# Sandwich of attention and channel mixing on one core: the gate read out of PSUM one slot sooner, ahead of the low plane of probabilities, its statistics and power one slot sooner too

## The reference

```
def ln(x): return (x - mean(x)) / sqrt(var(x) + 1e-5)

# attention, full 2048 x 2048 scores per batch
n = ln(x)
qkv = n @ weight_qkv         # bands 0:64 and 192:256 of the 256 in float16, 64:192 in float32
q, k, v = split(qkv); q = q / 16
y = softmax(q @ k.T) @ v
x = x + ln(y @ out_w.T + out_b)

# channel mixing
n = ln(x); prev = n shifted down by one row, zeros in the first
r = sigmoid((mu_r * n + (1 - mu_r) * prev) @ W_r.T)
k = square(relu((mu_k * n + (1 - mu_k) * prev) @ W_k.T))
x = x + ln(r * (k @ W_v.T))
```

## Time and profile before

| | |
|---|---|
| median of 3 runs | 855.45 us (854.24 to 855.83) |
| the profiled execution, its own time | 853.94 us |
| its span in the trace | 851.8 us |
| TensorE busy | 794.6 us, 93% |
| VectorE busy | 712.5 us, 84% |
| GpSimd busy | 550.8 us, 65% |
| ScalarE busy | 508.5 us, 60% |

### The profile page before, as it was taken

How to read it: one execution, slowest core, us unless ns; L and a number is a source line. 1 busy time by engine, 2 the same in 40 slices (tenths; PEclk the granted TensorE clock), 3 DMA queues, 4 the chain that set the end, 5 groups by cost and what they waited for, 6 DMA issues and landing times.

```text
span 851.8 us, 16118 instructions
## 1 busy us (share of the span) xinstructions
PE 794.6 (93%) x5749; PEld 572.5 (67%) x5749; DVE 712.5 (84%) x1805; ACT 508.5 (60%) x639; POOL 550.8 (65%) x717
## 2 busy tenths in 40 slices
PE   4879999999999999999999999999999999998664
PEld 3536767677776777677776776777777777777542
DVE  5698989988899998988889998988888888874553
ACT  3475556566566557766656557666666656655341
POOL 2110245677668777777768767777777777788761
PEclk9999999999999999999999999999999999999865
DMA  7565777477756864686648756775456646585100
GB/s 179 112 148 107 161 174 147 101 145 150 150 88 166 172 143 110 134 155 147 133 93 169 166 137 130 137 155 131 106 111 136 119 109 108 137 157 139 41 25 26
DMA packets 369312, 109.72 MB, mean 129 GB/s; under 512 B 342992, under 2 KB 368976, under 8 KB 369232
## 3 DMA queue, kind: packets, MB, share of 16 engines
q1 hardware_dynamic: 369232, 108.69, 61.0%
HBM read 18.75 MB, written 8.39 MB: 32 GB/s over the span
## 4 chain that ended last, share of the span: by engine, by line
PE 52%; DVE 30%; issue 8%; POOL 5%; ACT 2%; DMA 1%; SPq 1%; DVEq 0%; POOLq 0%; ACTq 0%
DVE probs L849 7%; PE M L1058 4%; PE M L1060 4%; PE M L1059 4%; PE S L1090 4%; PE S L1091 4%; PE S L1092 4%; PE S L1093 4%; PE S L1094 4%; PE Y L1111 4%; PE Y L1112 4%; PE Y L1113 4%; PE Y L1114 4%; PE Y L1115 4%; DVE p_lo L865 3%
## 5 line engine op out<-in xcount | busy, mean ns | idle before, releaser
L849 DVE TENSOR_SCALAR_CACHE_REDUCE probs<-S 128x512 f32<-128x512 f32 x256 | 173.2, 677 | 29.7 <-PE S L1094 29.5
L647 ACT ACTIVATE probs<-probs,exp_bias,kappa 128x2048 f32<-128x2048 f32 x64 | 133.6, 2088 | 51.3 <-DVE exp_bias L860 50.8
L865 DVE TENSOR_TENSOR p_lo<-probs,p_hi 128x2048 f16<-128x2048 f32 x64 | 151.5, 2367 | 3.1 <-ACT p_hi L597 3.1
L1112 PE MATMUL Y<-pt_lo,planes 128*128 128x256 f16 x512 | 140.2, 274 | 0.0
L1111 PE MATMUL Y<-pt_hi,planes 128*128 128x256 f16 x512 | 140.2, 274 | 0.0
L1113 PE MATMUL Y<-pt_hi,planes 128*128 128x256 f16 x512 | 140.2, 274 | 0.0
L1114 PE MATMUL Y<-pt_lo,planes 128*128 128x256 f16 x512 | 140.1, 274 | 0.0
L1115 PE MATMUL Y<-pt_hi,planes 128*128 128x256 f16 x512 | 140.0, 273 | 0.0
L597 ACT ACTIVATE p_hi<-probs 128x2048 f16<-128x2048 f32 x64 | 121.5, 1899 | 21.8 <-DMA pt_lo<-p_lo 21.8
L1090 PE MATMUL S<-turned,q_hi 128*128 128x512 f16 x256 | 97.9, 382 | 8.2 <-DVE q_lo L840 5.1
L541 POOL TENSOR_TENSOR xm_lo<-mixed,xm_hi 128x512 f16<-128x512 f32 x62 | 99.9, 1611 | 4.2 <-ACT xm_hi L597 4.1
(11 more groups left out here) (184 smaller groups left out, 2005.9 us busy)
## 6 DMA issues: line engine op xcount, KB each, us to landing
x_res<-in_L_attn_x SPq DMA_DIRECT2D x32, 256.0 KB, 3.0
out_x<-gate SPq DMA_DIRECT2D x32, 256.0 KB, 2.3
xs<-in_L_attn_x SPq DMA_DIRECT2D x28, 128.0 KB, 2.9
xs<-in_L_attn_x SPq DMA_DIRECT2D x14, 256.0 KB, 3.3
pt_hi<-p_hi SPq DMA_TRANSPOSE x64, 4.0
pt_lo<-p_lo SPq DMA_TRANSPOSE x64, 4.0
mxt<-mx SPq DMA_TRANSPOSE x31, 3.3
pt_hi<-in_L_attn_weight_qkv SPq DMA_DIRECT2D x3, 128.0 KB, 2.6
```

What stands on the lines that cost most here:

```text
L647: act.activation(probs[:, h % 2, t, :], probs[:, h % 2, t, :], ACT.Exp, bias=exp_bias[:, t:t + 1], scale=kappa[:, 0:1], accum_out=row_sum[ ...
L849: dve.tensor_scalar(probs[:, h % 2, t, c * BLK:(c + 1) * BLK], S[k % RING][:, :], 1.0, None, ALU.mult, ALU.max, accum_out=chunk_max[:, t, ...
L865: dve.tensor_tensor(p_lo[:, t, :], probs[:, h % 2, t, :], p_hi[:, t, :], ALU.subtract).then_inc(p_lo_made, 1)
L1112: pe.matmul(to[:, 0, :], low, p_l, start=False, stop=final, skip_group_check=True)
```

## The change

The constants of three stages become smaller by one, and the call of `gated` moves up in VectorE's list from behind the low squares to a place ahead of `probs_low`. `gate_norm`, `finish` and the store stay where they were.

```diff
     FEED = 58
-    GATE = 60
-    GATE_STATS = 61
-    GATE_RSQRT = 62
+    GATE = 59
+    GATE_STATS = 60
+    GATE_RSQRT = 61
     GATE_NORM = 62
...
                 if (h := at(k, Y_LOW)) is not None:
                     attended_low(h)
+                if (h := at(k, GATE)) is not None:
+                    gated(h)
                 if (ht := exp_at(k, FIRST_LOWER, LOWER)) is not None:
                     probs_low(*ht)
...
                 if (h := at(k, SQUARE_LOW)) is not None and h >= DRAIN:
                     squares_low(h)
-                if (h := at(k, GATE)) is not None:
-                    gated(h)
                 if (h := at(k, GATE_STATS)) is not None:
                     gated_stats(h)
```

## The result

The changed kernel takes 858.04 us (median of 20 executions, 854.17 to 859.38), the kernel before 853.62 us (20 executions on the same chip, 851.21 to 855.83). The ratio is 1.0052, 95% interval 1.0041 to 1.0063: 4.4 us slower, where I had forecast 13.3 us faster. The time lies outside my range, on the side that I gave 5 in 100. All medians of this document are over fast executions; one of the six executions of the kernel "old order in the drain" took 4688 us and is not among them.

The account below looks back on a forecast made before the run. Bound: PE, losing 9.1 us in the 17 half-units with preparation, mainly to gate waits, plus long drain waits. 8.5 us there and 4.8 in the drain gave 13.3, so 855.45 to 842.2 us; stated range 839.0 to 850.5 (0.83).

Parts of the forecast that it names:

- What bounds the kernel: 17 half-units with preparation take 412.00 us where 402.9 would do: 9.1 us lost, mainly PE waiting for the gate.
- Part one: Gate ahead of tile 0's p_lo on VectorE: ends 3.0 us sooner, gap to the receptance 3.5 us instead of 0.5.
- Part two: Statistics and power sooner: gshift ahead of tile 1's p_lo, 3.6 us sooner; VectorE's 1.58 us wait before y_lo goes.
- What it costs: Power ahead of L520 and differences on GpSimd: 0.75 us VectorE cost per half-unit against 0.7 room; gain taken as 8.5.
- the third rival: L520 and L526 both ahead of tile 1's p_lo, 2.2 us per half-unit: 10.7 us slower, 866; chance 0.05.
- The drain: From slot 256 on, shorter PE waits and a faster clock: 4.8 us gain, bounds 2.7 and 8.5.
- The two waits that I had counted on: Project waits at slots 265 and 281: first to gain 2.3 us; second, together with slot 285's gate wait, 2.3.
- term (d): Drain receptance waiting 1.17 us for xm_lo: either gains 1.2 us or loses 0.6, taken as 0.
- Term (e): Drain: with shorter pauses fewer PE matmuls run at the slow clock, gain taken as 0.2 us.
- the drain gives nothing: Drain waits for the gate may turn into waits for xm_lo or rrstd: 847.0 us; chance 0.13.
- signs for "right": No gate waits before slot 256, half-units at 23.70 us, gshift 0.2 to 0.3, no y_hi wait, shorter drain project waits.
- signs for "wrong": Tile 1's p_lo over 3.2 us, PE waits at scores or project, half-units over 24, or rrstd waits over 1 us.

Follow-up runs that it names:

- old order in the drain: Changed kernel with GATE_RSQRT back at 62, and gate and statistics at their old place from half-unit 24 on: 847.0 us, ratio 0.9921 to the kernel before.
- the version with the power kept: Changed kernel with only GATE_RSQRT back at 62, so gate and statistics move but the power does not: 846.35 us, ratio 0.9918 to the kernel before.
- The two kernels above that keep this order and leave work out: Changed kernel with 2 of 256 columns of GpSimd's differences made: 845.1 us; changed kernel with 1408 of 2048 columns of tile 0's p_lo made: 847.1 us.
- power alone: Kernel before with only GATE_RSQRT at 61, the power ahead of mix_in_sum on GpSimd: 869.3 us, ratio 1.0188.

## Why the prediction was wrong, step by step

**What bounds the kernel: right.** 17 half-units, 9.1 us lost, and 402.9 us as the least: the version with the power kept has exactly that.

**Part one: right.** The receptance's matmul started at 622.96 in the steady half-unit, the gate was done at 619.47, 3.5 us ahead as forecast.

**Part two: the chain right.** gshift started 5.7 us behind the gate, where I had 6.0, took 0.20 us, and ScalarE did not wait for it there any more; p_lo of tile 1 started 7.4 us behind the gate, where I had 7.5. What I didn't say is what GpSimd does until its moments come: nothing, for 4.32 us.

**What it costs: this step failed**, in two terms. I had written 0.9 us of loss at tile 1 less 0.16 us won at tile 0, 0.75 against 0.7 us of room, and taken nearly the full gain. The loss at tile 1 came out smaller, 2.86 - 2.29 = 0.57 us. The gain at tile 0 was a loss of 3.11 - 2.47 = 0.64 us. Of this p_lo I had said in part one that it is 0.68 us later and that its readers are far off; I had not asked what GpSimd would start in those 0.68 us. I had read it in a half-unit without preparation, where xt is the neighbour, and carried it over to the 17 in which xm_lo is. Then the operations that GpSimd does later: L908 (21.0 - 15.8) / 17 = 0.30 us, L916 0.12. Together 1.63 us. The busy time of the stretch shows a little less: 400.4 - 378.2 = 22.2 us, and one p_lo more, of 2.7 us, starts 0.15 us behind its end: 1.31 to 1.46 us per half-unit. With that my own sum comes near: 22.2 to 24.9 us of cost less 12.8 us of room is 9.4 to 12.1 us of lag on 402.9, 412.3 to 415.0; measured 413.0. The 12.8 us, though, are 17 times 0.75, the figure of the cost; the room that I had worked out was 1.45 - 0.76 = 0.69 us, 11.8 us in the 17, and with it the sum gives 413.3 to 416.0.

It is the third rival, the port that takes more than the gate gave, by another pair of operations than I named there. Of L520 and L526, both in front of p_lo of tile 1, the second is there and the first is not, as I had argued; in its place stands xm_lo, at tile 0, for which I had no term. I let this rival decide only from 1.6 us per half-unit; that point held a gain of 4.8 us in the drain, and without it, it is (12.8 + 9.1) / 17 = 1.29 us.

The Trainium skill (SBUF — State Buffer, Who interferes with whom) says that the order of issue decides who stands. The races here agree: where xm_lo starts 0.03, 0.25 or 0.63 us ahead, the p_lo of tile 0 takes 3.28, 3.06 or 2.69 us, that is each time 2.28 and what is left of the first 1.03 us of an xm_lo. At the shortest lead a trace no longer shows who is first: in three kernels of this study an xm_lo seen 0.03 us ahead took 3.33 us, and the p_lo its 2.28 or 2.29.

**The drain: wrong.** I forecast 4.8 us of gain; the profile shows 2.0 us of loss from slot 248 on. The two waits that I had counted on did shrink, from 3.23 to 0.85 us and from 3.98 to 2.08 us, as I had said. But the time came back at other doors. The timeline of PE in the drain, to be read against the earlier trace rows:

```profile
759.09 0.28 PE L1058 MATMUL M<-wt_hi,xm_hi 128*128 128x256 f16 x1 [2.44 <-POOL xm_lo L541]
...
767.19 0.28 PE L1058 MATMUL M<-wt_hi,y_hi 128*128 128x256 f16 x1 [0.85 <-DVE y_lo L869]
...
777.49 0.28 PE L1058 MATMUL M<-wt_hi,xm_hi 128*128 128x256 f16 x1 [1.88 <-POOL xm_lo L541]
...
793.46 0.28 PE L1058 MATMUL M<-wt_hi,xm_hi 128*128 128x256 f16 x1 [1.52 <-POOL xm_lo L541]
...
799.52 0.38 PE L1058 MATMUL M<-wt_hi,y_hi 128*128 128x256 f16 x1 [2.08 <-DVE y_lo L869]
...
810.73 0.37 PE L1058 MATMUL M<-wt_hi,xm_hi 128*128 128x256 f16 x1 [6.08 <-DVE gate L924]
```

The xm_lo of term (d), which I had put at 0, came behind p_lo and cost 1.3 us more (2.44 for 1.17); two waits for xm_lo, 1.88 and 1.52 us, are new, and the last one for the gate is 6.08 us instead of 4.50. What is late ahead of the second of these is seen on VectorE and GpSimd:

```profile
784.57 1.54 DVE L908 TENSOR_SCALAR att<-res,rmv,rrstd 128x256 f32<-128x256 f32 x2 [1.10 <-POOL rrstd L483]
786.03 2.67 DVE L916 SCALAR_TENSOR_TENSOR mixed<-diff,mu,xt 128x256 f32<-128x256 f32 x2
```

```profile
783.82 0.71 POOL L483 TENSOR_TENSOR rrstd<-rvar,minus_half 128x2 f32<-128x2 f32 x1
784.51 1.46 POOL L551 TENSOR_TENSOR gate<-gate,res 128x256 f32<-128x256 f32 x2
785.92 1.20 POOL L546 TENSOR_TENSOR sq_lo<-square,sq_hi 128x512 f16<-128x512 f32 x1
```

rrstd is late, L908 stands for it, and as it and `finish` are released at the same moment they run on top of each other, and so on down both lists. Term (e), the clock, gave more than the 0.2 us that I took: from slot 248 on the same 680 matmuls keep PE busy 90.4 us instead of 93.7, at a mean granted clock of 0.87 instead of 0.83. PE's idle time took it back, 37.1 us instead of 31.7. This is the rival "the drain gives nothing", by the wait for rrstd that I had named in it. The reading is of one profile. The two kernels above that keep this order and leave work out come to 123.7 and 124.8 us, below the 125.4 of before. How much of the 2.0 us is the drain's own spread stays open, and so does the source of this spread.

**What would show it.** Of the signs for "right" came the gate waits (but for two of 0.27 us), the short gshift, no wait of VectorE for y_hi before the drain, and the project waits of the drain. Of the signs for "wrong" came two: waits of PE at the scores (q_lo) and at the project (0.55 us), and half-units over 24 us (27.1). The p_lo of tile 1 was longer, but at most 3.0 us and not over 3.2, and the wait for rrstd did not come before the drain. A sign on VectorE's whole busy time would have caught it at once: 400.4 of 413.0 us.

## What to carry to other kernels

A move of 0.7 us on a full engine has two prices beside its own time: what the neighbour engine starts in the gap that it opens, and, if an operation is moved up to where its input is not there yet, everything behind it in its queue, which moves down. Price each of them in every kind of stretch (with and without preparation), and leave the waiting to the engine that has time (here GpSimd, 285 of 403 us busy) by keeping its long operations under the full engine's long ones. The two prices show in different ways: a lost race as more busy time of the full engine, a displaced queue as waits (power alone: both p_lo unchanged, and 1.9% slower). The better half of this change is to keep `GATE_RSQRT = 62`: 846.35 us, 0.8% under the kernel before and 1.3% under the changed one.

## What the runs showed of the hardware

- Length does not protect: an operation of 128x2 elements that starts inside a p_lo is held to its end. The carry copy took 2.25 us at 626.86 (0.18 us where no p_lo runs), gshift 2.27 us for 0.20. For GpSimd's chains of four tiny operations this is more than all their work. A memset of the same 128x2 elements, which reads nothing, is not held: 0.10 us at 289.23 in the changed kernel, inside the p_lo that runs from 288.75 to 291.44.
- The outcome turns on some tenths of a us (p_lo 0.35 us ahead before, xm_lo 0.26 us ahead now, in the half-unit shown): a 0.68 us operation in front of p_lo made 17 races out of 17 go to xm_lo, of which it had won 4 before. Who loses pays the rest of the winner's time: 0.4 to 1.0 us if it is p_lo, 1.7 to 2.05 us if it is xm_lo (2.89 to 3.20 for 1.15). The sum of the two is smaller when the short one wins; it only falls on the engine that has no room.
- In these traces a busy time grows without more work: an engine that is shut out is shown as busy. VectorE's 45.2 us more in the changed kernel have no other work behind them.
